# Normalising on ScalarE in the long convolution, and fp32 transposes split at eviction at the head of two layers, in an eight-layer gated block on one core

## The reference, cut to what matters

```python
# x: (16, 128, 256), fp32; the layers are applied in turn, each gated by tanh(g)
x = x + tanh(g_xattn[0]) * long_convolution(ctx, ctx, layernorm(x), ssm_kernel, D, 8)
x = x + tanh(g_ffn[0])   * moe_64_experts_top8_plus_shared(layernorm(x), ...)
x = x + tanh(g_xattn[1]) * rms_attention(layernorm(x), ctx, ...)
x = x + tanh(g_ffn[1])   * moe_8_experts_top2_plus_shared(layernorm(x), ...)
x = x + tanh(g_xattn[2]) * quantised_attention(layernorm(x), ctx, ...)
x = x + tanh(g_ffn[2])   * quantised_ffn(layernorm(x), ...)
x = x + tanh(g_xattn[3]) * causal_attention(layernorm(x), ctx, ctx)
x = x + tanh(g_ffn[3])   * ternary_ffn(layernorm(x), ...)
# layernorm(x) = (x - mean) / sqrt(var + 1e-5), over the 256 columns
```

## Time and profile before

| | us |
|---|---|
| median of three runs | 2691.83 |
| lowest and highest run | 2687.53, 2692.05 |
| time of the profiled execution | 2689.27 |
| its span, first to last instruction | 2687.5 |
| PE busy | 2115.3 (79%) |
| DVE busy | 1977.0 (74%) |
| ACT busy | 1512.2 (56%) |
| POOL busy | 852.1 (32%) |

### The profile page before, as it was taken

The page is one execution under the profiler, slowest core; times in us unless marked ns, Lnnn a source line. Parts: engine busy times, 40 slices in busy tenths (PEclk is TensorE's granted clock), DMA queues, the critical chain, the costliest instruction groups (busy, mean ns, idle before and its releaser), DMA issues. The chain is left out here.

```text
span 2687.5 us, 53376 instructions
## 1 busy us (share of the span) xinstructions
PE 2115.3 (79%) x17577; PEld 1191.3 (44%) x17577; DVE 1977.0 (74%) x3727; ACT 1512.2 (56%) x2756; POOL 852.1 (32%) x726
## 2 busy tenths in 40 slices
PE   4748999999968689998557888888888853498555
PEld 2335656565546447885332333333333331266323
DVE  6885655555555784335768999999999968688887
ACT  3435533333367653332348999999999932355332
POOL 5720000000035250004106677677777621111000
PEclk9769999999979899999655555555555566687656
DMA  6352222112140441222103554445445410100000
GB/s 196 80 204 67 66 67 66 66 62 70 59 134 2 151 160 45 68 56 82 39 2 71 91 91 91 93 92 92 91 91 93 91 37 22 32 0 0 32 8 23
DMA packets 377434, 193.82 MB, mean 72 GB/s; under 512 B 305515, under 2 KB 348779, under 8 KB 375147
## 3 DMA queue, kind: packets, MB, share of 16 engines
q1 hardware_dynamic: 374189, 183.16, 27.0%
q0 software_dynamic: 3072, 8.39, 1.0%
HBM read 95.25 MB, written 23.09 MB: 44 GB/s over the span
## 5 line engine op out<-in xcount | busy, mean ns | idle before, releaser
L2209 ACT ACTIVATE qa_e<-qa_S,qa_nb,qa_sq 128x512 uint8<-128x512 f32 (+1 forms) x805 | 709.2, 891 | 15.3 <-DVE qa_nb L2224 8.9
L2220 DVE TENSOR_REDUCE qa_mx<-qa_S 128x1 f32<-128x512 f32 x1024 | 636.9, 682 | 25.3 <-PE qa_S L2175 23.2
L2175 PE MATMUL qa_S<-qa_kT,qa_qb 128*128 128x512 f16 x1024 | 534.6, 609 | 115.1 <-ACT qa_e L2209 104.5
L2151 POOL CAST qa_pT<-qa_eT 128x2048 bf16<-128x2048 uint8 x256 | 483.6, 1891 | 209.7 <-DMA qa_eT<-qa_e 156.3
L2175 PEld LDWEIGHTS qa_S<-qa_kT,qa_qb 128*128 128x128 f16 x1024 | 89.8, 106 | 455.4 <-ACT qa_e L2209 439.9
L969 PE MATMUL moe_G<-hT,moe_W 128*128 (+1 forms) x792 | 193.7, 381 | 7.1 <-DVE moe_zero L937 7.1
L978 PE MATMUL moe_O<-moe_W,moe_ap 128*128 (+1 forms) x1584 | 194.5, 273 | 4.1 <-DVE moe_ap L933 4.1
L2184 PEld LDWEIGHTS qa_O<-qa_V,qa_pT 128*128 128x128 bf16 x4096 | 162.2, 107 | 74.6 <-issue 66.5
L969 PE MATMUL moe_U<-hT,moe_W 128*128 (+1 forms) x792 | 192.9, 380 | 0.0
L909 ACT ACTIVATE moe_ap<-moe_a 128x512 f16<-128x512 f32 x132 | 83.1, 629 | 194.4 <-DVE moe_a L931 194.4
L1112 POOL MEMSET rms_nothing<- 128x512 f16 x1 | 0.5, 524 | 588.5 <-POOLq L2973 588.5
(11 more groups left out here) (425 smaller groups left out, 3638.9 us busy)
## 6 DMA issues: line engine op xcount, KB each, us to landing
moe_wb<-weights_T SPq DMA_DIRECT2D x264, 128.0 KB, 2.8
moe_W<-in_moe_w SPq DMA_DIRECT2D x40, 384.0 KB, 11.6
moe_W<-in_moe_w SPq DMA_DIRECT2D x11, 1152.0 KB, 17.6
moe_xs_rows<-rms_nothing SPq DMA_DIRECT2D x46, 128.0 KB, 1.9
moe_ys_rows<-moe_ys SPq DMA_DIRECT2D x23, 256.0 KB, 2.1
conv_rows<-conv_parts SPq DMA_DIRECT2D x16, 256.0 KB, 2.9
qa_eT<-qa_e SPq DMA_TRANSPOSE x256, 3.1
conv_qst<-conv_rows SPq DMA_DIRECT2D x96, 32.0 KB
```

The costliest lines, as they stand in the source:

```text
L2151: nc.gpsimd.tensor_copy(pT[:, u % RING, :, :].rearrange("p (b r) q -> p b r q", r=2), pairs).then_inc(s_cast, 1)
L2175: nc.tensor.matmul(S[:, bank(m), :], qb[:, g // 2, j, g % 2, :], kT[:, g, q * QW:(q + 1) * QW], start=True, stop=True).then_inc(s_S, 1)
L2209: nc.scalar.activation(e8[:, u % RING, q * QW:(q + n) * QW], S[:, b:b + n, :].rearrange("p b c -> p (b c)"), ACT.Exp, bias=nb[:, u % 2:u % ...
L2220: nc.vector.reduce_max(mx[:, i, q:q + 1], S[:, bank(m + q), :], axis=AXX).then_inc(s_mx, 1)
```

## The change

In the convolution DVE no longer normalises. It makes a second per-token number beside the reciprocal, `shift` = -mean * rstd, for a quarter at a time (`scales`), and ACT makes H = rstd * X + shift in `queries`, ahead of the high part. In the two heads `Layernorm` and `Transposed` are replaced by `NormTransposed`.

```diff
@@ long_convolution, ScalarE
                 def queries(c):
+                    act.wait_ge(s_shift, c + 1)
+                    for t in range(c * Q, c * Q + Q):
+                        nc.scalar.activation(sh.H[:, t, :], sh.X[:, t, :], ACT.Identity, bias=shift[:, t:t + 1],
+                                             scale=rstd[:, t:t + 1]).then_inc(s_norm, 1)
                     act.wait_ge(s_norm, c * Q + Q)
                     nc.scalar.activation(parts[:, 0, quarter(c), :], sh.H[:, quarter(c), :], ACT.Copy).then_inc(s_qhi, 1)
@@ long_convolution, VectorE
-                def normalise(c):
+                def scales(c):
                     dve.wait_ge(s_std, c + 1)
                     nc.vector.reciprocal(rstd[:, quarter(c)], std[:, quarter(c)]).then_inc(s_rstd, 1)
                     dve.wait_ge(s_rstd, c + 1)
-                    for t in range(c * Q, c * Q + Q):
-                        nc.vector.tensor_scalar(sh.H[:, t, :], sh.X[:, t, :], mv[:, t, 0:1], rstd[:, t:t + 1],
-                                                ALU.subtract, ALU.mult).then_inc(s_norm, 1)
+                    nc.vector.scalar_tensor_tensor(out=shift[:, quarter(c)], in0=mv[:, quarter(c), 0], scalar=-1.0, in1=rstd[:, quarter(c)],
+                                                   op0=ALU.mult, op1=ALU.mult).then_inc(s_shift, 1)
@@ quantised_attention
-                norm = Layernorm(nc, head, sh, "qa_ln")
-                run(nc, Transposed(nc, head, sh, "qa_hT", norm), LoadSplit(nc, head, items, "qa_load"))
+                run(nc, NormTransposed(nc, head, sh, "qa_hT"), LoadSplit(nc, head, items, "qa_load"))
@@ program, mixture
-                    norm = Layernorm(nc, head, sh, f"moe{layer}_ln")
-                    hT = Transposed(nc, head, sh, f"moe{layer}_hT", norm)
+                    hT = NormTransposed(nc, head, sh, f"moe{layer}_hT")
```

More of the change, by code:

```diff
@@ L165, in long_convolution @@
         rstd = sb("rstd", [P, NB])
+        shift = sb("shift", [P, NB])
         rows = nc.dram_tensor("conv_rows", [4, NB, P, D], F16, kind="Internal").ap()
@@ L171, in long_convolution @@
         s_stack = [sem("stack0"), sem("stack1")]
-        (s_toepload, s_dvals, s_zero, s_anti, s_toep, s_khi, s_klo, s_qhi, s_qlo, s_stats, s_mv, s_std, s_rstd, s_norm, s_vpad, s_S, s_c, s_Ad, s_Ap,
+        (s_toepload, s_dvals, s_zero, s_anti, s_toep, s_khi, s_klo, s_qhi, s_qlo, s_stats, s_mv, s_std, s_rstd, s_shift, s_norm, s_vpad, s_S, s_c, s_Ad, s_Ap,
          s_Y, s_res) = map(sem, (
-             "toepload", "dvals", "zero", "anti", "toep", "khi", "klo", "qhi", "qlo", "stats", "mv", "std", "rstd", "norm", "vpad", "S", "copied",
+             "toepload", "dvals", "zero", "anti", "toep", "khi", "klo", "qhi", "qlo", "stats", "mv", "std", "rstd", "shift", "norm", "vpad", "S", "copied",
              "Ad", "Ap", "Y", "res"))
@@ L339, in _ @@
                 statistics(0)
-                normalise(0)
+                scales(0)
                 low(0)
@@ L360, in _ @@
                             if g == 3:
-                                normalise(c)
+                                scales(c)
                             if g == 6:
```

## The result

The changed kernel takes 2674.75 us (median of 4 runs, 2671.52 to 2678.08) against 2690.27 us for the kernel before beside it: ratio 0.9946, 95% interval 0.9933 to 0.9958. It is faster, by some 15 us and not by the 24.8 us of the forecast: the ratio forecast was 0.9908 (2667.0 to 2691.83). On the 2691.83 us that the forecast started from, the measured ratio makes 2677.3 us, above its 2657 to 2675; that 2674.75 itself lies just inside is owed to the lower time of the kernel before. The profiled execution is the one of 2678.08 us, its span 2676.4 us.

The account below looks back on a forecast made before the run. DVE was taken to bound both heads, with waits around `normalise` and PE's clock in the convolution. Gains 8.0 + 7.8 + 7.6 = 23.4 us from 2689.27 give 2665.9; a run-mean correction makes 2667.0, range 2657 to 2675.

Parts of the forecast that it names:

- The mixture's head: First mixture: the new head takes 17.09 us on DVE instead of 25.08, and the router's logits shift whole; 8.0 us gained.
- The quantised attention's head: Quantised attention: ACT reaches the split of `cT` 16.03 us after the head's start instead of 23.9; 7.8 us gained.
- The convolution: Convolution: normalising on ACT instead of DVE frees DVE and shortens PE's waits around the quarters; 7.6 us gained, wide bounds.
- 2.7 + 2.6 + 2.6 - 0.3: Convolution: us gained in quarters 1, 2 and 3, less the loss in quarter 0; sum 7.6 us.
- On DVE each quarter loses four operations and gains one of 0.16 us: Convolution, each quarter: the added DVE operation was priced at 0.16 us by the same operation in rms attention.
- they are twice as slow where POOL works too: Convolution: DVE's four normalisations take 4.59 us in tile 0, against 2.02 in quarter 0, because POOL works beside them.
- no work beside it: Convolution, quarter 0: on the way to the first scores nothing runs alongside, so the edit loses 0.3 us there.
- For quarter 1 the same walk: Convolution, quarter 1: following the engines from 34.56, the values there start 2.7 us before 43.83.
- If the clock falls twice as now: Convolution: with PE's clock falling twice as before, it ends at about 145.6 us instead of 153.2.
- ACT as the new wait: Rival, convolution: ACT's normalisation is stretched or copies for POOL come late, so its 7.6 us vanish; 2674.6 us, chance 0.12.
- The clock stays up: Rival, convolution: PE's clock does not fall, up to 8 us more gained; 2659.0 us, or 2663 if once; chance 0.18.
- The cited port rule: Convolution: VectorE's two-port modes and GpSimd exclude each other, ScalarE has own ports, so ACT's normalisation keeps 2.08 us.

Follow-up runs that it names:

- after: Profiled execution of the changed kernel (both new heads and the convolution's edit), against the kernel before: 2678.08 us; the kernel's median 2674.75 us, ratio 0.9946.
- columns: Shift made by four one-column DVE operations instead of one instruction: in the changed kernel ratio 0.9931 to the kernel before, with the convolution's edit alone 0.9999.

## Why the prediction was wrong in size and right in direction

- **The mixture's head, 8.0 us: right**, measured 8.0 with the DMA engines at a share of 0.94; the quantised head, at 0.51, took the same 17.1 us. ACT had its expert weights in time.
- **The quantised attention's head, 7.8 us: right**, measured 7.9. Both were priced by the rows of the same helper doing the same work in rms attention. All four executions with the new heads and without extra matmuls or late loads have the logits 28.4 us after their head's start and `cT` after 15.9 or 16.0.
- **The convolution, 7.6 us: wrong**, measured as 0 (1.0001, with 2.4 us to either side). Its terms 2.7 + 2.6 + 2.6 - 0.3 came out as 0.1, 1.8, 1.4 and about 0. The 3.3 us that are left are lost again between the boundaries; the clock agrees with that, but that the edit causes it is not shown, and this part of the cause stays open. Four steps of the walk failed.
  - "On DVE each quarter loses four operations and gains one of 0.16 us". The row is from rms attention, where POOL at that moment fills an array and reads nothing; here POOL is multiplying. The prediction had used that very difference for the removed operations (2.02 against 4.59 us in the earlier trace rows) and not for the added one. Measured in after: 0.93 to 1.67 us. With columns the boundaries give 2.5 and 2.2 us each, near the forecast 2.6; with the one instruction 1.8 and 1.4. It cost 1.5 us over these two.
  - "they are twice as slow where POOL works too". None of the four normalisations was: two waited for POOL's products to end and two took their 0.40 us. The same holds where the prediction saw "no work beside it": in quarter 0 POOL multiplies until 11.98 us, the first normalisation takes 1.06 us, and in the changed kernel the shift 0.93. The low part started 1.0 us later there and not 0.3; the first scores started at 25.1 us all the same, with the edit and without it (means of four).
  - "For quarter 1 the same walk", 2.7 us. The walk followed the engines to the next values and stopped there; the stacks of tile 2, which every execution waits for, land no earlier, for the loads keep the DMA engines full until 46 us. This term was 2.7 and measured 0.1.
  - "If the clock falls twice as now". It fell twice, but for 47.8 us in place of 27.4, after a first rise at 63.2 and not 47.3. Holding the clock of one execution fixed was the error: with the old convolution the lower level's share varies by 24 us, which is 8 us of time, as much as the term itself.
- **The rivals.** *ACT as the new wait* named the wrong engine: the normalisation kept 2.08 us. That its time, 2674.6, is nearly what came out (2674.75) is luck: it came by another road. *The clock stays up* did not occur: it fell at 76.9 although no gap of PE after 71 was longer than 1.05 us, PE working for 2.88 of 5.80 us, where the forecast leaned to a fall. By the Trainium skill (TensorE: Matmul & The Clock Gate, "HAM oscillation — how this bites in real kernels") long gaps are what to avoid; here the absence of long ones did not suffice. In the run with extra matmuls, PE busy for 91.99 of 100 us, the level stayed at 1.00.
- **The cited port rule.** The sentence drawn from the Trainium skill (SBUF — State Buffer, "Who interferes with whom") was right for ACT, which kept its 2.08 us. It named VectorE's two-port modes alone. The same section says that VectorE and GpSimd share a pair of ports under an exclusive lock, and that a VectorE instruction with two SBUF inputs contends with a GpSimd instruction that reads SBUF, not with one that only writes it. The trace agrees: the shift ended with POOL's instruction each of four times, for instance 72.36 and 72.34, and took 0.16 us beside the memset. The section was read for the engine that gained work and not for the instruction that stayed behind.
- **The time behind the convolution.** The 5.2 us that the profiled execution gains after 1302 us are no effect of the change: in three executions of the kernel before, the stretch from the start of the quantised head to the end takes 1414.6, 1411.8 and 1408.5 us. In after it takes 1401.6, with the head's 7.9 us added 1409.5, which lies among them.

## What to carry to other kernels

Price an instruction by a row in which the neighbours are busy with the same things: a tiny one can cost what is left of the neighbour's instruction, here up to 1.70 us for 0.16. Look at the instructions of a group one by one and not at their sum. Follow a walk through waits to the next *transfer* that hangs on it, and look whether that one was waiting for you. And where one execution's clock carries the estimate, look at several before, since its share of the time may be as large as the edit.

## What the runs showed of the hardware that was not expected

- A DVE instruction of 128x4 elements with two SBUF inputs took 0.93 to 1.70 us beside a GpSimd tensor product, until that one ended, and 0.16 us with GpSimd idle or beside its memset; four of 128x1 with one tensor input and a scalar column took 202 to 215 ns each beside the same product.
- A DVE `tensor_scalar` of 128x256 fp32 took 0.40 us alone; beside GpSimd products the first two of four took 1.81 and 2.21 us, each ending 0.14 to 0.15 us after a product, and the last two 0.40.
- TensorE's clock in the same kernel, from one execution to the next: first rise at 37.8, 47.3 and 50.9 us, time at the lower level in the convolution 40.6 to 57.1 us.
- 200 independent matmuls at the start raised the clock at 8.3 us; it was down again by 22 us, before the first real matmul at 26.18, after PE had stood still from 16.6 us on.
